# Latent attention loop of a two-layer decoder: key turns and the denominators' product put between a score group's third and fourth unit, reciprocals and context product put later

## The reference, cut to what matters

```python
q_hk = (hidden_q @ Wq.T).reshape(b, s, H, K)
q_big = jnp.einsum('bshk,hkq->bshq', q_hk, w_kc_q)
kv_rope = kv_c * cos[None] + _rotate_half(kv_c) * sin[None]
q_r = jnp.einsum('bshq,hqr->bhsr', q_big, W_qr)
k_r = jnp.einsum('bld,hdr->bhlr', kv_rope, W_kr)
scores = jnp.einsum('bhsr,bhlr->bhsl', q_r, k_r)
attn = jax.nn.softmax(scores, axis=-1)
ctx_c = jnp.einsum('bhsl,bld->bhsd', attn, kv_rope)
ctx_lat = jnp.einsum('bhsd,hkd->bshk', ctx_c, w_kc_kv)
out = ctx_lat.reshape(b, s, H * K) @ Wo.T
```

## Time and profile before

| | us |
|---|---|
| median of 3 runs | 1872.93 |
| lowest and highest | 1871.71 and 1884.01 |
| the profiled execution | 1873.22 |
| its span, first to last instruction | 1871.5 |

### The profile page before, as it was taken

The page is one execution under the profiler, slowest core; times in us unless marked ns, Lnnn a source line. Parts: engine busy times, 40 slices in busy tenths (PEclk is TensorE's granted clock), DMA queues, the critical chain, the costliest instruction groups (busy, mean ns, idle before and its releaser), DMA issues. The chain is left out here.

```text
span 1871.5 us, 40366 instructions
## 1 busy us (share of the span) xinstructions
PE 1467.8 (78%) x13805; PEld 930.2 (50%) x13820; DVE 1393.7 (74%) x2385; ACT 1068.7 (57%) x1820; POOL 652.1 (35%) x654
## 2 busy tenths in 40 slices
PE   1677776999999999999997466861687759956892
PEld 0455553444444444444447356761465547735782
DVE  6888874799999998888876773326789646667674
ACT  1777763777777776777763342431567435535461
POOL 1222212165555645454510254551333110027242
PEclk9655665999999999999998677985899779958896
DMA  6920000112212121212110153433000010024334
GB/s 157 332 104 1 1 1 33 37 34 56 60 46 69 46 67 49 63 53 64 52 26 2 40 159 121 136 109 109 1 1 0 1 26 1 0 87 135 100 106 157
DMA packets 93389, 123.67 MB, mean 66 GB/s; under 512 B 22945, under 2 KB 74217, under 8 KB 92867
## 3 DMA queue, kind: packets, MB, share of 16 engines
q1 hardware_dynamic: 83395, 98.88, 18.7%
q0 software_dynamic: 7776, 21.28, 3.2%
q10 hardware_dynamic: 2112, 2.10, 0.3%
HBM read 66.85 MB, written 40.30 MB: 57 GB/s over the span
## 5 line engine op out<-in xcount | busy, mean ns | idle before, releaser
L2643 DVE TENSOR_TENSOR lat_dsum<-lat_dsum,lat_Pb 125x896 f32<-125x896 f32 x320 | 481.5, 1505 | 43.0 <-ACT lat_Pb L2588 33.7
L2588 ACT ACTIVATE lat_Pb<-banks 125x896 f32<-125x896 f32 x384 | 329.2, 928 | 145.2 <-PE banks L2477 130.8
L2455 PE MATMUL banks<-lat_Pb,lat_kv 125*64 125x448 f32 x1536 | 306.5, 541 | 0.0
L2477 PE MATMUL banks<-lat_QH,lat_kT 64*125 64x448 f16 x1536 | 247.7, 363 | 5.0 <-DVE lat_QT L2613 2.1
L2477 PEld LDWEIGHTS banks<-lat_QH,lat_kT 64*125 64x125 f16 x1536 | 104.6, 133 | 139.3 <-issue 66.3
L2455 PEld LDWEIGHTS banks<-lat_Pb,lat_kv 125*64 125x64 f32 x1536 | 100.6, 137 | 146.4 <-issue 138.3
L2409 POOL TENSOR_TENSOR lat_kk<-lat_rot,lat_kk 125x768 f16<-125x768 f32 x32 | 66.9, 2090 | 265.3 <-ACT lat_kk L2547 265.3
L2978 POOL DMA_INDIRECT sent_outputs<-moe_yb,moe_yidx x98 | 99.4, 1014 | 135.9 <-ACT moe_yb L3235 107.7
L2477 PE MATMUL banks<-lat_QL,lat_kT 64*125 64x448 f16 x768 | 136.0, 351 | 0.0
L3116 PE MATMUL banks<-moe_w2d,moe_gT 88*128 (+3 forms) x780 | 106.1, 288 | 22.6 <-DVE moe_gT L3453 15.6
L3116 PEld LDWEIGHTS banks<-moe_w2d,moe_gT 88*128 88x128 f16 (+1 forms) x780 | 77.5, 103 | 39.6 <-issue 27.0
(11 more groups left out here) (446 smaller groups left out, 3256.8 us busy)
## 6 DMA issues: line engine op xcount, KB each, us to landing
moe_xb<-sent_rows SPq DMA_DIRECT2D x49, 257.0 KB
lat_raw<-in_ctx_dram SPq DMA_DIRECT2D x32, 375.0 KB
sent_rows<-zero SPq DMA_DIRECT2D x1, 7453.0 KB, 49.0
lat_QH<-lat_QT SPq DMA_DIRECT2D x64, 112.0 KB, 2.9
lat_QL<-lat_QT SPq DMA_DIRECT2D x64, 112.0 KB, 5.0
lat_rD<-lat_reciprocals SPq DMA_DIRECT2D x62, 112.0 KB, 2.8
moe_arena<-sent_outputs SPq DMA_DIRECT2D x12, 512.0 KB, 6.5
sent_rows<-zero SPq DMA_DIRECT2D x1, 5140.0 KB, 65.1
```

The lines of the kernel that those rows point to most:

```text
L2455: ins = nc.tensor.matmul(ps[u * DC:(u + 1) * DC, 6, 0:8 * T], kv[:, par, tt, :], Pb[:, tile_slot(tt, par), u, :], start=tt == 0, stop=tt = ...
L2477: ins = nc.tensor.matmul(ps[0:KP, n % 3 * 2 + q, 0:8 * T], kT[rows, par, 2 * pair + low, 0:KP], Q[rows, par, 8 * u:8 * u + 8, :].rearrange ...
L2588: nc.scalar.activation(Pb[:, slot:slot + 2, u, :], ps[0:KP, n % 3 * 2:n % 3 * 2 + 2, 0:8 * T], ACT.Exp, scale=1.0 / QSCALE).then_inc(exp_d ...
L2643: ins = nc.vector.tensor_tensor(dsum[:, par], dsum[:, par], Pb[:, tile_slot(tt, par)], ALU.add)
```

## The change

Four things are put elsewhere; no instruction is added to or taken from the arithmetic.

- On TensorE, the key turns of groups 0 and 2 stand between the third and the fourth score unit of their group, and the denominators' product of tile b-1 moves from the end of group 0 to the same place in group 1.
- On ScalarE, the copy of the denominators stands after exponential 7 (before: 4), and `rows` after exponential 8 (before: 7).
- On VectorE, the reciprocals of tile b-1 stand behind add 9 (before: 6).
- On VectorE, the context product of tile b-1, which stood behind add 10 of body b, becomes `kept_context`, behind add 3 of body b+1. The last one stands behind the loop.

```diff
@@ tensor, body @@
-                            for pair in (2 * g, 2 * g + 1):
-                                for u in range(2):
-                                    scores(b, par, pair, u)
+                            for pair, u in ((2 * g, 0), (2 * g, 1), (2 * g + 1, 0)):
+                                scores(b, par, pair, u)
                             if g == 0:
                                 turn(b, par, 1)
+                            if g == 1 and past(b, 1):
+                                denominators(b - 1, (par + 1) % 2)
                             if g == 2 and live(b + 1, B):
                                 turn(b + 1, (par + 1) % 2, 0)
+                            scores(b, par, 2 * g + 1, 1)
                             for tt in range(4 * g - 4, 4 * g):
                                 if g:
                                     values(b, par, tt)
                                 elif past(b, 1):
                                     values(b - 1, (par + 1) % 2, KT + tt)
-                            if g == 0 and past(b, 1):
-                                denominators(b - 1, (par + 1) % 2)
@@ scalar, body @@
-                            if n == 7 and live(b + 1, B):
+                            if n == 8 and live(b + 1, B):
                                 rows(b + 1, (par + 1) % 2)
-                            if n == 4 and past(b, 1):
+                            if n == 7 and past(b, 1):
                                 keep_denominators(b - 1)
@@ vector @@
+                    def kept_context(b):
+                        dve.wait_ge(pv_kept, b + 1)
+                        dve.wait_ge(rec_in, 32 * b + 32)
+                        context(b, pv[:])
...
                             ins.then_inc(summed, 1)
-                            if tt == 6 and past(b, 1):
+                            if tt == 3 and past(b, 2):
+                                kept_context(b - 2)
+                            if tt == 9 and past(b, 1):
                                 reciprocals(b - 1)
-                            if tt == KT - 2 and past(b, 1):
-                                dve.wait_ge(pv_kept, b)
-                                dve.wait_ge(rec_in, 32 * b)
-                                context(b - 1, pv[:])
 
                     over_tiles(dve, body, 0, n=B)
+                    kept_context(B - 2)
```

## The result

The changed kernel takes 1928.63 us (median of 4 runs, 1927.96 to 1929.89), beside 1872.32 for the kernel before (4 runs with it, 1869.42 to 1884.01): ratio 1.0296, interval 1.0255 to 1.0337. It is 56 us slower. The forecast was 1924, 51 us more than before. The profiled execution has a span of 1926.9 us, 55.4 more than that of before.

The account below looks back on a forecast made before the run. VectorE was taken to bound the latent loop up to about 730 us; its 18.48 us plus a 2.25 us gap make 20.73 us a tile. With +48.4 in the loop and +2.1 at the end, +51 on 1873.2 gives 1924 us, range 1893 to 1943.

Parts of the forecast that it names:

- The forecast mechanism: Latent loop: ScalarE's copy waits for the later product in the one pv tile, delaying VectorE and TensorE; chance 0.64.
- The walk: One tile from the product's end through ScalarE's copy and exponentials 4 and 5: VectorE's add 4 starts at 2.25 us.
- VectorE's work of 18.48 us: VectorE's full work per latent tile where it doesn't wait, all collisions with GpSimd included: 18.48 us.
- The first held copy: ScalarE's copy of context sums in tile 2, forecast at 415.3 where it stood at 411.25: +4.0 us.
- the last step: The latent loop's last tile, without rotations beside it, forecast at 18.3 us.
- the sum: Latent loop: 415.3, 28 steps of 20.73 and 18.3 give 1014.0 (+48.4); end +2.1; total +51 us.
- (a): TensorE's key turns before the fourth unit cover its wait, worth up to 0.25 us three times a tile.
- (b): TensorE's denominators inside the second score group no longer wait for VectorE's last add: 0.41 us.
- The other chain: TensorE and ScalarE from exponential 4 to the next tile's exponential 3: 1 us of room, alone 18.3 us.
- rival 2: GpSimd's first rotation falls into VectorE's gap: period 19.4, 37 us less, 1887 us; half of it 1905; chance 0.12.
- rival 1: TensorE's clock falls on most tiles: period 21.3 us, 16 us more, 1940 us; chance 0.13.
- Rival 3: ScalarE's stop doesn't bind as the product is made when the sums are; VectorE's 18.48 us decides: 1855 us; chance 0.06.

Follow-up runs that it names:

- e1: The changed kernel with two pv tiles, so ScalarE's copy waits for the product of one tile earlier: 1868.87 us beside 1865.21, ratio 1.0008.
- e9: The changed kernel with the kept context product behind add 2 and the reciprocals behind add 8: 1872.68 us beside 1846.81, ratio 1.0144.
- e2: The changed kernel with the kept context product behind add 1 and the reciprocals behind add 7: 1865.46 us beside 1865.21, ratio 0.9990.
- e4: The kernel before with only the VectorE part (reciprocals behind add 9, kept product behind add 3): 1926.47 us beside 1865.21, ratio 1.0313.
- e3: The kernel before with only the TensorE and ScalarE parts of the change, VectorE as before: 1878.55 us beside 1865.21, ratio 1.0046.
- e5: The changed kernel with SP's load of context rows issued earlier, two tiles ahead: 1893.88 us beside 1846.34, ratio 1.0267.

## Why the prediction was right

**The forecast mechanism.** It was right, and every link was shown: the copy waits for the product (first row of the waits), VectorE waits for exponentials 4 and 5, TensorE for exponential 4; undoing the wait alone (e1) undoes the loss, moving the product one and two adds earlier (e9, e2) takes 1.1 us and then 1.9, all of the loss, off the step, and the VectorE part alone (e4) brings it.

**Its size.** The walk gave 2.25 us of gap; measured are 2.32 and 2.38 in turn. VectorE's work of 18.48 us stayed. The step came out at 20.8 us (29 steps from 416.54 to 1019.83, 603.3 us), against 20.73. The first held copy stood at 416.54 instead of 415.3, as the last add of tile 1 began near 410.2 and not at 409.0; the last step took 18.7 instead of 18.3. The 28 steps between were 20.88 us each where the sum has 20.73: 0.10 by the gap of 2.35, the rest by the clock (below). At the end the kept product waited 2.90 us for `rD`, and the reciprocal L2669 started 17.2 us after the last copy (18.0 forecast, 15.9 before). The timeline there, all engines:

```profile
1019.83 0.54 ACT L2559 ACTIVATE lat_pv<-banks 128x448 f32<-128x448 f32 x1 [2.50 <-DVE lat_QT L2628]
...
1035.40 0.62 DVE L2628 TENSOR_TENSOR lat_QT<-lat_pv,lat_rD 128x448 f32<-128x448 f32 x1 [2.90 <-DMA lat_rD<-lat_reciprocals]
...
1037.07 2.96 DVE L2669 RECIPROCAL lat_rD<-banks 128x448 f32<-128x448 f32 x1
```

In sum, +5.3 before the first held copy (4.0 forecast), +49.0 over 29 steps (44.4), +1.3 at the end (2.1): 55.6 against 51.

**Parts (a) and (b): wrong by a term.** "Together TensorE could come down to 18.2 us a tile" failed. The waits of 0.25 and 0.41 us did go, but the step of TensorE alone is 18.95 us (e1, e2, e3), more than the 18.74 of the old order when nothing is late. I had taken the moved blocks' cost as the same in either place, and left out the changes of kind. The total didn't show it, since TensorE waits in the changed kernel anyway: 1.2 to 2.0 us per tile before the fourth unit, where I had expected 2 to 3; 20.8 less 18.95 is 1.85.

**The other chain: wrong by 2 us.** "This chain has 1 us of room, and alone it would give 18.3 us" left out L2409's collision (1.44 us) and the changes of kind (some 0.5 us: exponential 3 ends 15.9 to 16.0 us behind the product in e5, 15.5 in the walk): 18.3 + 1.44 + 0.5 = 20.2, and e5 shows 20.27. The room was 0.5 us. So it was luck, not working, that this chain stayed under the forecast period: another 0.6 us on it would have set the period. For the same reason rival 2's price of 37 us was wrong: its mechanism is real (e5), but the second chain leaves it 10.7.

**The clock (rival 1).** It fell in 4 of 29 tiles, at 418, 544, 732 and 920 us, not in most. Such a step took 22.0 us and the one behind it 20.25, together 0.6 us more than two others: some 2.5 us in all. I had put nothing in the sum.

**Rival 3** could not come: the copy was released by the product in all 30 held tiles, and by TensorE only in the first. e1 shows what it would have been worth, and that is no gain that can be told: TensorE's 18.95 us take over from VectorE's 18.48. My 1855 for it was too low by 29 x 0.47 = 14 us in the steps alone; by e1's ratio it would be 1874.

## What to carry to other kernels

When a consumer is moved later, look for who must wait until its buffer is free, and what stands behind that one in its queue; with a single buffer, the move of the product by four adds turned 0.77 us of slack into a gap on the engine that sets the rhythm, and a second buffer or two adds behind the product undo it. Filling a small hole in TensorE with a block of another kind pays only if the hole is larger than what the two borders of the block cost: here holes of up to 0.25 us did not pay. After finding the bound, work out the next chain with all of its collisions too: it sets what a cure is worth.

## What the runs showed of the hardware

In these traces a block of matmuls of another kind costs TensorE 0.05 to 0.15 us on each side; whether the kind of product or something else at the border of a block takes it, no run separates. By the starts of the matmuls in e1 and before, a score unit takes 0.57 us ahead of another unit and 0.66 ahead of turns or denominators; eight transposes 0.24 us ahead of values and 0.33 ahead of scores; sixteen matmuls of values 3.01 us ahead of the denominators (fp32 like them) and 3.15 ahead of scores.

In the changed kernel TensorE's clock fell to the lower level of 1.2 GHz at 4 of 29 standstills, which lasted 1.75 us (before 543.03), 1.80, 1.92 and 2.04 us; all 29 lasted 1.2 to 2.0. In its second run it fell at 3 of 29. In e4, with 1.4 to 3.0 us, it fell at 7 of 29, all of 2.2 us or more, but not at one of 2.82 us. In e5, with 1.1 to 1.3 us, it fell at none of 28, and once at the first stop of 3.65 us. The values in such a stretch took 4.92 us instead of 3.23. The Trainium skill (TensorE: Matmul & The Clock Gate, the summary of rules) lets the clock fall behind longer idle stretches than these; here the trace decides against it.

The Trainium skill (SBUF — State Buffer, on who interferes with whom) says that a VectorE instruction with two inputs in SBUF and a GpSimd instruction that reads SBUF lock each other out for the whole of one. The trace of the changed kernel agrees where GpSimd was first: VectorE's product took 2.07 us with L2409 beside it (581.78) and 0.61 without (603.86). For the other direction it has L2409 itself, which took 2.44 us where it began 0.94 us before the end of an add (580.93) and 1.80 us where some 0.3 us of an add were left (601.18).
